# Attention over eight batches: VectorE's evictions, quad copy and norm in another order, and a modulation in two halves

## The reference, cut to what matters

```python
q = rms_norm(x, qn_scale) @ q_w.T + q_b
k = rms_norm(x, kn_scale) @ k_w.T + k_b
v = x @ v_w.T + v_b
q = apply_rotary(q, cos, sin); k = apply_rotary(k, cos, sin)
weights = jax.nn.sigmoid(einsum('bhqd,bhkd->bhqk', q, k) * scale)
weights = weights / (jnp.sum(weights, axis=-1, keepdims=True) + EPS_RENORM)
attn = einsum('bhqk,bhkd->bhqd', weights, v)
return attn.reshape(B, L, D) @ o_w.T + o_b
```

## Time and profile before

| | us |
|---|---|
| median of three executions | 1639.29 |
| the profiled execution | 1638.98 |
| its span in the profile | 1637.2 |
| sigmoid 0 of batch 1 to sigmoid 0 of batch 7 | 681.88 to 1040.71 |
| busy PE / PE weight load / DVE / ACT / POOL | 1479.5 / 1182.1 / 1139.5 / 930.2 / 416.1 |

### The profile page before, as it was taken

One profiled execution on the slowest core, in us unless ns is written; L12 is line 12 of the kernel. 1 busy time (PEld: TensorE's weight loads), 2 busy tenths in 40 slices (PEclk: granted clock), 3 DMA queues, 4 the chain that ended last, 5 costly groups with the idle time before them and its releaser, 6 DMA issues. The chain is left out here.

```text
span 1637.2 us, 29233 instructions
## 1 busy us (share of the span) xinstructions
PE 1479.5 (90%) x10406; PEld 1182.1 (72%) x10406; DVE 1139.5 (70%) x2334; ACT 930.2 (57%) x1172; POOL 416.1 (25%) x413
## 2 busy tenths in 40 slices
PE   6899999869999977889989989875999999999998
PEld 4788888757788764445445545444889999999987
DVE  4577777568788785575685675545557878787868
ACT  2566665435555534775575575652337777777752
POOL 1122322330010021222143233222213333333330
PEclk9899999979999997999999899896999999999999
DMA  7000000210000000400000000003227888888864
GB/s 271 1 1 0 0 0 0 78 41 1 0 0 0 0 26 1 157 2 1 4 25 18 15 25 18 18 21 137 82 85 210 235 233 234 232 235 230 236 161 154
DMA packets 65455, 130.51 MB, mean 80 GB/s; under 512 B 8249, under 2 KB 38754, under 8 KB 64866
## 3 DMA queue, kind: packets, MB, share of 16 engines
q1 hardware_dynamic: 51074, 110.37, 21.4%
q0 software_dynamic: 14304, 19.15, 5.7%
HBM read 97.50 MB, written 32.00 MB: 79 GB/s over the span
## 5 line engine op out<-in xcount | busy, mean ns | idle before, releaser
L1821 ACT ACTIVATE at_wide<-at_sc_ps 128x2048 f32<-128x2048 f32 x128 | 240.5, 1879 | 121.8 <-PE at_sc_ps L1657 120.2
L2270 POOL DMA_INDIRECT sums<-e_y,e_row_ids x78 | 121.6, 1559 | 249.3 <-ACT e_y L2425 237.4
L52 PE MATMUL e_gate_ps<-e_h_parts,e_w 128*128 128x256 f32 (+1 forms) x1128 | 177.0, 304 | 7.5 <-DVE e_w L2479 4.0
L2479 DVE TENSOR_TENSOR e_w<-e_raw,e_w 128x1024 fp32r<-128x1024 f32 x123 | 147.3, 1223 | 44.2 <-ACT e_w L2378 44.2
L52 PE MATMUL e_up_ps<-e_h_parts,e_w 128*128 128x256 f32 (+1 forms) x1128 | 175.3, 303 | 0.0
L52 PEld LDWEIGHTS e_gate_ps<-e_h_parts,e_w 128*128 128x128 f32 x1128 | 155.4, 194 | 15.3 <-DVE e_w L2479 4.1
L52 PEld LDWEIGHTS e_up_ps<-e_h_parts,e_w 128*128 128x128 f32 x1128 | 155.5, 193 | 7.7
L1671 PE MATMUL at_o_ps<-at_wide,at_v_ones 128*32 128x512 f32 x1024 | 143.0, 631 | 0.0
L2378 ACT ACTIVATE e_w<-e_raw 128x1024 fp32r<-128x1024 f32 x123 | 125.3, 1048 | 7.2 <-DMA e_raw<-in_experts 7.2
L2335 PE MATMUL e_down_ps<-e_w,e_hidden 128*128 128x256 f32 x936 | 127.9, 286 | 1.3 <-DVE e_hidden L2528 1.3
L1657 PE MATMUL at_sc_ps<-at_qT,at_kT 32*128 32x512 f32 x1024 | 97.4, 455 | 32.2 <-ACT at_wide L1821 29.9
(11 more groups left out here) (351 smaller groups left out, 2754.6 us busy)
## 6 DMA issues: line engine op xcount, KB each, us to landing
e_raw<-in_experts SPq DMA_DIRECT2D x123, 512.0 KB
e_rows_in<-slots SPq DMA_DIRECT2D x39, 272.0 KB
sums<-shared SPq DMA_DIRECT2D x17, 256.0 KB
x<-in_L_attn_x SPq DMA_DIRECT2D x8, 512.0 KB, 9.4
gate<-gates SPq DMA_DIRECT2D x4, 1024.0 KB
slots<-shared SPq DMA_DIRECT2D x15, 272.0 KB
out<-x SPq DMA_DIRECT2D x7, 512.0 KB, 2.9
e_sums<-sums SPq DMA_DIRECT2D x4, 512.0 KB, 4.3
```

What stands on the lines that cost most here:

```text
L52: last = pe.matmul(out, left(i), right(j), start=n == 0, stop=n == len(steps) - 1)
L1821: nc.scalar.activation(wide[:, u % 2, :], sc_ps[:].rearrange("p n s -> p (n s)"), ACT.Sigmoid, scale=float(HD) ** -0.5).then_inc(sig_done, 1)
L2270: pool.indirect_dma_start(c.sums_dram[:, :], bass.IndirectOffsetOnAxis(ap=row_ids[:, j % 2, t:t + 1], axis=0), y[:, j % 2, t, :], None, co ...
L2479: nc.vector.tensor_tensor(w[:, buf, REST, q], raw[:, q], w[:, buf, HEAD, q].bitcast(F32), ALU.subtract).then_inc(w_split, 1)
```

## The change

Three edits, all in `attention_part`.

1. **DVE's order** in each iteration. `keep_by_feature` of tile 0 goes ahead of `moments`; the copy of the third quad (`keep_quad(b, 2)`) goes ahead of `add_turned` of tile 3; `normalise` goes from ahead of that copy to between `keep_by_feature` of tile 2 and of tile 3.
2. **ACT's modulation** in two halves where a next batch follows: the first chunk stays behind sigmoid 15, the second, which signals `next_done`, goes behind sigmoid 0 of the next batch.
3. **PE's scores** of the first quad wait for the key tile that they read instead of for all four.

```diff
                     if u == 0:
                         pe.wait_ge(qT_kept, NT * (b + 1))
-                        pe.wait_ge(kT_kept, NT * (b + 1))
+                    if u < NT:
+                        pe.wait_ge(kT_kept, NT if is_first(b) else NT * b + u + 1)
...
-                def modulate(b):
+                def modulate(b, ks=range(KC)):
                     act.wait_ge(c.start, 1)
                     act.wait_ge(xT_done, b + 1)
-                    for k in range(KC):
+                    for k in ks:
...
-                    last.then_inc(next_done, 1)
+                    if KC - 1 in ks:
+                        last.then_inc(next_done, 1)
...
                         if past and u == 15:
-                            modulate(b - 1)
+                            modulate(b - 1, range(1) if coming else range(KC))
+                        if b >= 2 and u == 0:
+                            modulate(b - 2, range(1, KC))
...
                     keep_quad(b, 1)
+                    if coming:
+                        keep_by_feature(n, 0)
                     if past:
                         moments(p)
                     if coming:
-                        keep_by_feature(n, 0)
                         keep_by_feature(n, 1)
                     divide_quad(b, 1)
                     if coming:
                         rotate(n, 2)
                         add_turned(n, 2)
                         rotate(n, 3)
+                    keep_quad(b, 2)
+                    if coming:
                         add_turned(n, 3)
+                        keep_by_feature(n, 2)
                     if past:
                         normalise(p)
-                    keep_quad(b, 2)
                     if coming:
-                        keep_by_feature(n, 2)
                         keep_by_feature(n, 3)
```

## The result

The changed kernel took **1611.2 us** (median of four executions, 1608.9 to 1612.4), against 1639.0 for the kernel before: ratio 0.983, 95% interval 0.981 to 0.985. The forecast was 1620 with a range of 1614 to 1628. The direction was right, the size too small: 27.8 us gained where 19 were forecast. One execution of e_p3_1, a kernel further down, took 1841.6 us at a mean granted clock of 0.73 and stands outside every median and ratio; all others ran at 0.94 to 0.96.

What follows compares the result with a forecast made beforehand. It took the attention part as a loop of sigmoid, scores, sigmoid, lengthened by PE's work or waits. Six stretches falling from 140.85 to 121.8 us gain 19.05: from 1638.98 to 1619.9, said as 1620 us, range 1614 to 1628.

Steps and rivals of the forecast that it cites:

- Step A: Sigmoid 10 to 11: tile 0's query eviction ahead of `moments` frees PE's transposes of tile 1, gaining 1.18 us.
- Step B: DVE's chain from `rotate` of tile 2, without `normalise`: copy no longer waited for, sigmoid 15 in batch 4 3.3 us earlier.
- a sign of being wrong: In unit 12 or 13: a wait of PE for DVE beyond 0.6 us would show the forecast wrong.
- Step C: Ahead of `next_by_feature`: new 0.4 us wait for DVE; half of `modulate`, 0.67 us, gone before sigmoid 0.
- The stretches: Sigmoid 10 to the next batch's sigmoid 0, batches 1 to 6: 20.2 us each, 0.3 more in batches 3 and 6.
- POOL: Before tile 2's cosines: free 0.2 us late, hidden; as rival, `add_turned` delayed in batches 3 to 6, 1625.5 us, chance 0.07.
- The ranks: PE's ranks after sigmoid 0: `choose` on DVE ends later, its slack falling from 2.4 to 0.9 us, still enough.
- Edit 3: PE's scores of the first quad, wait by key tile: no gain found; bounds 0 and 0.7 us once, taken 0.
- the clock: Units 13 to 15: rival that PE's clock still falls in all six batches, 1.30 us each, 1627.5 us; chance 0.10.
- Slower: At `next_by_feature`: rival that tile 3's key eviction ends late; 5 us late loses 6.6 us, 1646 us; chance 0.02.
- more than that: Routing after unit 0: rival that shorter PE idle shortens the slow clock, 1.30 us four times, 1615 us; chance 0.08.

Runs made afterwards that it cites:

- e_p3_1: p3_copy_norm plus one more ScalarE copy of 128x512 between sigmoid 15 and `modulate` in batches 1 to 7; 1630.3 us.
- p3_copy_norm: Kernel before with only the copy of the third quad early and `normalise` late on DVE; 1619.8 us, ratio 0.988.
- p5_order: Kernel before with both DVE moves (tile 0's eviction; copy and `normalise`), `modulate` whole, no wait by key tile; 1616.1 us, ratio 0.986.
- p1_halves: Kernel before with only the modulation split in two halves; 1628.8 us, ratio 0.994.
- e_before_1: Kernel before plus one more ScalarE copy of 128x512 between sigmoid 15 and `modulate` in batches 1 to 7; 1643.1 us, ratio 1.002.
- d_before_6: Kernel before with six extra ScalarE copies of 128x512 ahead of sigmoid 0 of batch 0, to delay all of the attention; 1638.4 us, ratio 1.000.

## Why the prediction was wrong

*Step A (tile 0's eviction) was right.* 1.18 us a batch forecast, sigmoid 10 to 11 at 3.09 instead of 4.27; in batches 3 and 6, where an eviction of two instructions had been waited for, it was 1.44 and 1.74. The sum did not need these two gains, since it sets each new stretch against the old one.

*Step B (the copy and `normalise`) was right.* 3.3 us to sigmoid 15 with A's in it; measured 1.18 and 2.39, 3.6. Tile 3's transposes do set the end, with a wait of 0.62 us, and 1.1 and 1.4 in batches 3 and 6, more than the 0.6 that the prediction named as a sign of being wrong; the stretches came out as forecast even so. The slow clock of batches 4 to 6 in units 13 to 15 is gone: the granted clock is 1.00 in every window there. The wait for the copy is gone as well.

*Step C was right.* The new delay ahead of `next_by_feature` was put at 0.4 us and was 0.29 (in batches 3 and 6 some 0.5), and sigmoid 15 to 0 came to 3.01 us against 3.1 forecast. The half of `modulate` cost nothing behind sigmoid 0.

*The stretches:* 20.2 us forecast, 19.72 to 19.82 measured, and 20.54 and 20.80 in batches 3 and 6 against 20.5. Sum 120.4 against 121.8. *POOL* was late by 0.37 us at the cosines where 0.2 had been put, and hidden by `rotate`. *The ranks* did not wait for `choose`. *Edit 3* gained nothing, as forecast, but cost 0.09 us a batch, which the bounds of 0 and 0.7 us of gain had left out: the added waits had no price in the sum.

*Three rivals have slips in their sums,* none of which bears on the result. 1620 and 7.8 are 1628 for the clock, where 1627.5 stands, and 1620 and 5.6 are 1625.6 for POOL. In *Slower* the gain is said to be gone at 3.9 us late a batch; the sum's own gain is 3.2 us a batch, so that 5 us late would give 1650 and not 1646.

**The step that failed** is the one sentence on which the sum rested: "It all lies on the path: behind batch 7 everything starts earlier by as much", with the turns outside the stretches taken as they were. They were not. The six routing turns, 52.8 us in the kernel before, were not a fixed sum of work: each had 6.8 us of TensorE's lower clock in it, and how much it has changes with the rest of the batch. In the changed kernel three of them had 3.4 us, and that made the 5.1 us. The case was among the rivals ("more than that"), with a price of 5 us and a chance of 0.08; 5.1 us is what it gave. The size agrees by luck: the rival took four turns at 1.30 us, a price from units 13 to 15, and it was three turns at 1.6 to 2.1. And the mechanism named there, the idle time shortened by the half of `modulate`, does not carry it: p3_copy_norm gained 10.9 us in these turns without that half, and at one and the same idle time p3_copy_norm and p5_order took different steps. And the range ended at 1614, where the faster rival at 1615 and the forecast's own 3 us together reach 1612. Of the 8.1 us by which the fall of the span, 27.2, passed the 19.05 of the sum, 5.1 are these turns and 1.4 the stretches, less the 0.6 of the added waits. A further 2.2 us came in parts that the change does not touch, where the first sigmoid of the attention starts anywhere from 627.4 to 629.7 us in the kernels whose code ahead of it is the same.

What is shown: in batches 3 to 6 the routing turn takes 6.1 to 10.7 us with the same instructions, in steps that go with how long the lower clock stands in it; the changed kernel showed the same turns in two profiles; a delay of the whole leaves them as they are in batches 3 to 6 of the kernel before; and a change of 0.4 us a batch can change it by 10 us over the kernel in either direction. What stays open: what places the slow clock, and so which step a turn takes. The idle time of PE ahead of scores 1 does not decide it: at 1.14 us batches 3 and 4 of the changed kernel took 7.67 and 9.28 us, at 1.70 us p3_copy_norm took 7.7 and p5_order 9.2, and at 2.13 us the turns of e_p3_1 are on different steps. That it has some share in it is not ruled out: only runs with 1.9 us or more of it have a turn above 9.4 us. The Trainium skill says in TensorE: Matmul & The Clock Gate, Part 1, that the gate judges recent activity on a timing of its own, which does not start with the kernel. The runs neither show nor refute a timing of its own; that the same turns came out in two executions of the changed kernel, and that an offset of 2 us vanished within three batches, suggests that the batches fall into a pattern with the clock, but that is argued, not shown.

## What to carry to other kernels

When a wait is taken out of a loop, look beyond the wait for stretches of the same loop that run at TensorE's lower clock, and put them into the sum with both their values: here they gave 5 us on top of 20, and in other variants 9 us less (p1_halves) and 10 us more (e_p3_1), for changes of half a microsecond a batch. Their two values are best read from turns of the same code with more and with less of the lower clock, here 1.6 us apart in batches 3 to 6. A stretch without the waits in question, such as batch 0 here, is a good measure of what remains: it gave every one of the six stretches within 0.5 us. (No sum of durations was made to compare it with.) And try each edit of a bundle alone: one of the three did nothing but add a wait.

## What was not expected of the hardware

- With the same instructions the turn from sigmoid 1 to 2 took 6.1, 7.7, 9.2 or 10.3 to 10.7 us in batches 3 to 6 of the runs, by whether TensorE's granted clock was at its lower level for none of it, for 3.4 us, for 6.8 us or for longer.
- A uniform lengthening by one ScalarE copy (0.60 us alone, 0.4 us on the path) cost 3.3 us in one kernel (e_before_1) and some 10 us in another (e_p3_1); a delay of 2 us ahead of the loop (d_before_6) cost nothing.
- One more semaphore wait on PE, for a value long reached, went with 0.09 us more between two sigmoids, in each of seven batches and in all four profiles of kernels that had it; that the wait is the cause is not shown apart.
